# Fetching one of 112 gathered tiles row by row from the sync engine in a two-layer relational graph network

## The reference

```python
def rgcn_layer(x, src, dst, edge_type, w_rel, root, bias):     # N = 12500 nodes, E = 200000 edges, R = 10
    seg = dst * 10 + edge_type
    xs = x[src]                                                # one row of 128 floats for each edge
    sums = segment_sum(xs, seg, num_segments=N * 10)
    cnt = segment_sum(ones, seg, num_segments=N * 10)
    mean = (sums / maximum(cnt, 1.0)[:, None]).reshape(N, 10, 128)
    return einsum('nrd,rdo->no', mean, w_rel) + x @ root + bias

edge_type = argmax(edge_attr_42[:, 16:26], axis=1)
h = relu(rgcn_layer(x, src, dst, edge_type, w_rel1, root1, b1))
y = rgcn_layer(h, src, dst, edge_type, w_rel2, root2, b2)
out = layernorm(x + y)
```

## Time and profile before

| what | value |
|---|---|
| time, median of 3 runs | 3973.91 us (3973.23 to 3980.13) |
| the profiled execution's own time | 3973.67 us |
| its span, first to last instruction | 3972.0 us |
| busy share of the span: GpSimd, TensorE, VectorE, ScalarE | 75%, 67%, 47%, 9% |
| mean granted clock of TensorE | 0.819 of full speed |

### The profile page before, as it was taken

The page is one execution under the profiler, slowest core; times in us unless marked ns, Lnnn a source line. Parts: engine busy times, 40 slices in busy tenths (PEclk is TensorE's granted clock), DMA queues, the critical chain, the costliest instruction groups (busy, mean ns, idle before and its releaser), DMA issues.

```text
span 3972.0 us, 31733 instructions
## 1 busy us (share of the span) xinstructions
PE 2673.2 (67%) x10165; PEld 1797.6 (45%) x10166; DVE 1872.3 (47%) x2588; ACT 375.7 (9%) x399; POOL 2986.7 (75%) x3139
## 2 busy tenths in 40 slices
PE   4776777677677676777766666666666666666566
PEld 3444444444444444444454444444444444444444
DVE  6545545454554545555544343434434344443444
ACT  1010100101001010010100101010010100101010
POOL 7777777777777777777777777777777777777775
PEclk9787888878888888887888778788877878878788
DMA  4232232322323223232222222222222222222221
GB/s 132 75 88 84 78 94 78 90 79 78 94 78 94 74 78 94 78 88 67 80 67 61 66 62 63 62 65 62 63 63 65 63 62 62 65 62 63 64 64 52
DMA packets 151574, 293.69 MB, mean 74 GB/s; under 512 B 61619, under 2 KB 82503, under 8 KB 147958
## 3 DMA queue, kind: packets, MB, share of 16 engines
q0 software_dynamic: 100032, 205.07, 19.9%
q1 hardware_dynamic: 46630, 87.29, 6.7%
q10 hardware_dynamic: 4867, 0.79, 0.1%
HBM read 264.68 MB, written 28.25 MB: 74 GB/s over the span
## 4 chain that ended last, share of the span: by engine, by line
POOL 72%; issue 25%; PE 3%; POOLq 0%; DVE 0%; DMA 0%; ACT 0%; DVEq 0%
POOL rows L1400 71%; PE ps_agg L1820 1%; PE ps_agg L1817 1%; PE ps_out L1900 1%; PE ps_bc L1842 0%; DMA rows<-in_x_dram,idx_s 0%; POOLq L1436 0%; PE ps_agg L1900 0%; PE ps_out L1895 0%; DVE ring L2209 0%; DMA rows<-table,idx_s 0%; POOLq L1343 0%; POOLq L1430 0%; POOL mean L1396 0%; PE ps_out L1908 0%
## 5 line engine op out<-in xcount | busy, mean ns | idle before, releaser
L1400 POOL DMA_INDIRECT rows<-table,idx_s x1563 | 1481.7, 948 | 481.8 <-issue 481.8
L1400 POOL DMA_INDIRECT rows<-in_x_dram,idx_s x1507 | 1443.5, 958 | 459.3 <-issue 459.3
L1817 PE MATMUL ps_agg<-S_first,rows 128*128 128x390 f32 x1564 | 891.4, 660 | 1154.5 <-issue 727.9
L1820 PE MATMUL ps_agg<-S,rows 128*128 128x160 f32 (+2 forms) x4692 | 1241.1, 406 | 0.0
L2209 DVE TENSOR_TENSOR ring<-ps_agg,ring 128x429 f32 (+1 forms) x782 | 457.1, 585 | 1415.6 <-PE ps_agg L1820 696.7
L1820 PEld LDWEIGHTS ps_agg<-S,rows 128*128 128x128 f32 x4692 | 950.2, 242 | 347.7 <-issue 233.3
L1817 PEld LDWEIGHTS ps_agg<-S_first,rows 128*128 128x128 f32 x1564 | 336.5, 243 | 1397.2 <-issue 1022.8
L2195 DVE TENSOR_TENSOR S<-ps_iota,comb_b 128x1200 f32<-128x1200 f32 x392 | 547.5, 1397 | 0.0
L2253 DVE TENSOR_TENSOR mean<-ps_bc,ring 128x896 f32<-128x896 f32 (+2 forms) x284 | 300.7, 1060 | 490.8 <-PE ps_bc L1842 486.8
L1900 PE MATMUL ps_out<-mean,wall 128*128 128x448 f32 (+1 forms) x1120 | 507.9, 581 | 0.0
L1900 PEld LDWEIGHTS ps_out<-mean,wall 128*128 128x128 f32 x1120 | 228.9, 213 | 153.0 <-issue 143.9
(11 more groups left out here) (163 smaller groups left out, 814.6 us busy)
## 6 DMA issues: line engine op xcount, KB each, us to landing
attr<-in_edge_attr_dram SPq DMA_DIRECT2D x27, 1176.0 KB, 8.9
rows<-table,idx_s POOLq DMA_INDIRECT x1563, 2.5
rows<-in_x_dram,idx_s POOLq DMA_INDIRECT x1507, 2.5
x_in<-in_x_dram SPq DMA_DIRECT2D x54, 224.0 KB, 2.7
table<-h_s SPq DMA_DIRECT2D x54, 224.0 KB, 2.3
table<-outT SPq DMA_DIRECT2D x27, 224.0 KB, 3.7
xt_s<-table SPq DMA_DIRECT2D x27, 224.0 KB, 3.8
out_dram<-h_s SPq DMA_DIRECT2D x27, 224.0 KB
```

What stands on the lines that cost most here:

```text
L1400: pool.indirect_dma_start(out=rows[:, o, j, :], out_offset=None, in_=(x, table)[l][:, :], in_offset=bass.IndirectOffsetOnAxis(ap=at, axis= ...
L1817: ins = t_.matmul(sums, lhsT=rows[:, o, jj, :], rhs=S_first[:, PLACE[o], h, :, :], start=True, stop=False)
L1820: ins = t_.matmul(sums[:, :, lo:lo + w], lhsT=rows[:, o, jj, :], rhs=S[:, PLACE[o], h, j - 1, :].rearrange("p (r n) -> p r n", n=WN)[:, :, ...
```

## The change

For the first 13 laps of each layer the last tile of the lap, tile 7 of octet 6 in the odd half, is no longer gathered by GpSimd. The sync engine fetches it instead. A new function `fetch` runs four times in a lap, 32 rows each time, in a loop of four passes with eight rows a pass. A pass loads eight indices from `idx_sp` in SBUF into registers and issues eight DMAs. Each copies one row of 512 bytes from `x` or `htab` into `tile_d`, a scratch of 128 rows in DRAM. After the fourth part the sync engine waits until all 128 rows have landed, loads the whole scratch into `rows_sp` in SBUF, and loads the next lap's indices. TensorE takes this tile's weights from `rows_sp` and waits for `rows_sp_in` as well. The core of the diff:

```diff
+SP_OCT, SP_TILE, SP_LAPS, SP_UNIT, SP_PART = OCTS - 1, GT - 1, LAPS - 1, 8, 32
...
+        rows_sp = sb("rows_sp", [P, C])
+        idx_sp = sb("idx_sp", [1, P], I32)
...
+        tile_d = table2[60000:60000 + P, :]
...
+        def by_sync(b, par, o):
+            return par == 1 and o == SP_OCT and not is_(b, END)
...
-                            for j in range(GT - SHORT if is_(b, HALVES - 1) and o == OCTS - 1 else GT):
+                            for j in range(GT - SHORT if is_(b, HALVES - 1) and o == OCTS - 1 else
+                                           GT - 1 if by_sync(b, par, o) else GT):
...
+                def load_index(tile):
+                    sp.dma_start(idx_sp[0:1, :], src[bass.ds(tile * P, P)].rearrange("(a e) -> a e", a=1)
+                                 ).then_inc(idx_sp_in, 16)
+
+                def fetch(l, b, before, part):
+                    if isinstance(b, int) and b >= 2 * SP_LAPS:
+                        return
+                    if part == 0:
+                        landed = 8 * before + 16 * (1 - l)
+                        sp.wait_ge(idx_sp_in, landed if isinstance(b, int) else sp.snap(landed))
+                        if l or not is_(b, 0):
+                            sp.wait_ge(agg_ready[SP_OCT], before)
+                        if l and is_(b, 0):
+                            sp.wait_ge(rows_saved, 16 * PARTS)
+                        hold(b)
+                    with sp.Fori(part * SP_PART, (part + 1) * SP_PART - SP_UNIT + 1, SP_UNIT) as first:
+                        _, at = nc.values_load_multi_w_load_instructions(
+                            idx_sp[0:1, bass.ds(first, SP_UNIT)], engines=(SP_,), min_val=0, max_val=N - 1,
+                            skip_runtime_bounds_check_because=IN_ROWS)
+                        for e in range(SP_UNIT):
+                            sp.dma_start(tile_d[bass.ds(first + e, 1), :], (x, htab)[l][bass.ds(at[e], 1), :]
+                                         ).then_inc(row_copied[l], 16)
+                    if part == 3:
+                        copied = before * 1024 - l * (HALVES * 1024) + 1024
+                        sp.wait_ge(row_copied[l], copied if isinstance(b, int) else sp.snap(copied))
+                        hold(b)
+                        sp.dma_start(rows_sp[:, :], tile_d).then_inc(rows_sp_in, 16)
+                        if is_(b, 2 * SP_LAPS - 1):
+                            if l == 0:
+                                load_index(2 * HT - 1)
+                        else:
+                            load_index((b + 3) * HT - 1)
...
+                    fetch(0, b, before, 2 * par)
                     if not (isinstance(b, int) and b >= HALVES - 2):
                         sp.wait_ge(attr_used, with_it)
...
                         save_counts(b - 1, before)
+                    fetch(0, b, before, 2 * par + 1)
+                    if not is_(b, 0):
                         save_part(b - 1, 0, HN, before, h_s)
...
+                    fetch(1, b, before, 2 * par)
                     if not (isinstance(b, int) and b < 2):
                         save_out(b - 2, 0, HN, sp.snap(before - (HALVES + 1)) if not isinstance(b, int) else b - 1, o_s)
+                    fetch(1, b, before, 2 * par + 1)
                     sp.wait_ge(bc_ready[4], past)
...
+                            from_ = rows_sp[:, :] if by_sync(b, par, o) and jj == SP_TILE else rows[:, o, jj, :]
...
+                                    if par:
+                                        here = with_it * 8 - l * 16
+                                        pe.wait_ge(rows_sp_in, here if known else pe.snap(here))
```

More of the change, by code:

```diff
@@ L1117 @@
 DVE_ = mybir.EngineType.DVE
+IN_ROWS = "src names rows of x"
+SP_OCT, SP_TILE, SP_LAPS, SP_UNIT, SP_PART = OCTS - 1, GT - 1, LAPS - 1, 8, 32
+SP_ = mybir.EngineType.SP
 IN_RANGE = "the flag that chooses this path is computed from the same rows and bounds them"
@@ L1161, in gnn_kernel @@
         rows_in = [sem(f"rows_in{k}") for k in range(OCTS)]
+        row_copied = [sem(f"row_copied{l}") for l in range(2)]
+        rows_sp_in = sem("rows_sp_in")
+        idx_sp_in = sem("idx_sp_in")
         attr_max = sem("attr_max")
@@ L1567, in _ @@
                     load_late_src(o)
-                for b, before, with_it, par, past in halves(sp, 1, singly=1):
+                for b, before, with_it, par, past in halves(sp, 1, singly=2):
                     n = nodes_of(b)
+                    fetch(1, b, before, 2 * par)
                     if not (isinstance(b, int) and b < 2):
                         save_out(b - 2, 0, HN, sp.snap(before - (HALVES + 1)) if not isinstance(b, int) else b - 1, o_s)
+                    fetch(1, b, before, 2 * par + 1)
                     sp.wait_ge(bc_ready[4], past)
@@ L1819, in aggregate @@
                         else:
-                            ins = t_.matmul(sums[:, :, lo:lo + w], lhsT=rows[:, o, jj, :],
+                            from_ = rows_sp[:, :] if by_sync(b, par, o) and jj == SP_TILE else rows[:, o, jj, :]
+                            ins = t_.matmul(sums[:, :, lo:lo + w], lhsT=from_,
                                             rhs=S[:, PLACE[o], h, j - 1, :].rearrange("p (r n) -> p r n", n=WN)[:, :, 0:w],
@@ L1961, in _ @@
                             pe.wait_ge(S_ready[o], with_it)
-                            if o == OCTS - 1 and (l or last):
-                                gone = SHORT * 16 * (l + last)
-                                pe.wait_ge(rows_in[o], landed - gone if known else pe.snap(landed - gone))
+                            if o == OCTS - 1:
+                                if last:
+                                    gone = (l + 1) * (SHORT + SP_LAPS) * 16
+                                    pe.wait_ge(rows_in[o], landed - gone)
+                                else:
+                                    fixed = l * (SHORT + SP_LAPS) * 16 - l * HALVES * 8 - (1 - par) * 8
+                                    here = with_it * (P - 8) - fixed
+                                    pe.wait_ge(rows_in[o], here if known else pe.snap(here))
+                                    if par:
+                                        here = with_it * 8 - l * 16
+                                        pe.wait_ge(rows_sp_in, here if known else pe.snap(here))
                             elif l and is_(b, 0) and o < AHEAD:
```

## The result

The changed kernel takes 4039.62 us (median of 4 runs, 4038.61 to 4042.6) against 3976.26 for the kernel before in the same runs: 1.0162 times as long, 95% interval 1.0150 to 1.0174. It is 63 us slower; I had forecast it 33 faster, at 3941.

The account below looks back on a forecast made before the run. GpSimd, issuing gathers without pause, was taken to bound the kernel. Removing 13 gathers a layer saves 32.7 us from 3973.67, and the added work costs nothing: 3941 us predicted, own range 3937 to 3950, widened to 3936 to 3965.

Parts of the forecast that it names:

- The gathers do not get slower: Denies a rival: row copies beside GpSimd's gathers cost each 10 ns, 28 us of the gain, 3969 us; chance 0.05.
- Does it fit: Sync engine's work per lap against GpSimd's lap: 120 of 141.4 us in layer 0, 114 of 140.3 in layer 1.
- The row: One row copy on the sync engine: issue 0.475 plus 0.24 us for register instruction, moves and gaps, 0.71 in all.
- my limit of 31.7 for a part: Longest part of 32 rows that fits layer 0's lap: 31.7 us, a row of 0.88, an issue of 0.64.
- The old work: Sync engine's existing work in layer 0: 3.6 us for types and 2.1 for hidden rows each half, 11.4 a lap.
- 46 idle microseconds: TensorE idles about 46 us of each lap, so waiting 3.7 us for `rows_sp` once a lap was called free.
- the sum of 120: Sync engine in layer 0, per lap: four parts of 26.4 us plus 14.5 for old work, last landing and two issues.
- signs of being right: Gathers at 1.25 to 1.26 us, row issues 0.25 to 0.6, parts under 31, hidden-row stores slightly late, short `rows_sp` waits.
- the two of being wrong: GpSimd's sequencer waiting for TensorE in front of an octet; TensorE waiting tens of microseconds for `rows_sp`.
- the bounds: Limits for a row copy's issue on the sync engine: shortest plain issue 0.239 us, longest odd-shaped one 1.433.
- The sync engine becomes the bound: Rival: 128 row copies a lap decide from 0.88 us a row; 4441 us with an issue of 0.8; chance 0.14.
- TensorE's lateness comes back: Rival: TensorE over its 50 us makes GpSimd wait; 1.26 us a lap gives 3974, 2 gives 3993; chance 0.04.

Follow-up runs that it names:

- e9: The changed kernel with layer 0's attribute load issued behind the types' store and load back: 3943.31 us, ratio 0.9912 to the kernel before.
- e7: The changed kernel, but GpSimd gathers all 112 tiles, the sync engine's tile goes unused and part 0 waits for the scratch's readout: 3976.01 us, ratio 0.9998.
- e8: The changed kernel with the wait for octet 6 moved from part 0 to the load of `rows_sp`: 3983.78 us, ratio 1.0014 to the kernel before.
- e15: The changed kernel with each part's rows written out, only the source row from a register: 3936.67 us, ratio 0.9908 to the kernel before.
- e12: The changed kernel with rows copied straight into `rows_sp`, without scratch, on chips where the kernel before is slow: ratio 1.0459 to that kernel.
- e11: The changed kernel with rows written out into the scratch, on chips where the kernel before is slow: ratio 1.2092 to that kernel.
- e1: The changed kernel without row copies or scratch load, TensorE reading old rows, on slow chips: 4614 us against 4668 before, ratio 0.9881.

## Why the prediction was wrong

**What held.** GpSimd bounded the kernel, and the 26 gathers are worth what I said: 32.7 us forecast, 36.7 measured with direct copies (interval of the ratio 0.9893 to 0.9926, so 29 to 43). The DMA engines carry the packets without harm: queue q1 goes from 6.7 to 8.2% of their time, where I had 2% for the row copies. The gathers do not get slower, late types alone cost nothing, and in layer 1 the change does what was forecast.

**The step that failed is "Does it fit".** It added up the sync engine's work in layer 0 to 120 us a lap and held it against 141.4, the lap of 112 gathers, where the changed GpSimd has 111 and needs 140.1. The lap measured 147.9. Three terms make most of the difference, and the third is one of kind, not of size.

- The row. I took 0.71 us; it is 0.79 (issue 0.521 and not 0.475, register instruction 0.074 and not 0.06), and a part of 32 takes 29.4 and not 26.4: 12 us a lap. This alone stays under my limit of 31.7 for a part.
- The old work. I carried its 3.6 us for the types over unchanged, though its order had changed. The types' store now follows 32 row copies and the attributes at once, and the wait for it takes 5.0 instead of 1.3: 7.4 us a lap. e9 takes just this away.
- The closed circle. I let the tile be 3.7 us late and called it free, because TensorE has 46 idle microseconds and GpSimd gives it 50. I had part 0 wait "for the end of octet 6, about 1150", which is the old trace's 8 us of octet 6 behind 1142.3, although the line above it had the tile in SBUF only at 1146.0; and the sum of 120 has no term for this wait at all. But octet 6 itself waits for the tile that the parts bring. Once the tile is late, the wait is 5.4 us and moves along with the lateness, so it is a term of the sum, and the slack of TensorE does not pay for it. e7 and e8 take this one away.

With 120 + 12 + 7.4 + 5.4 the sum would have been 145, and about 3 us remain. Of the 147.9 four parts are 117.6, the waits for the types, the last row (13.2 / 11) and octet 6 are 10.0, 1.2 and 5.4, and 13.7 are left for the old issues with the holds and register instructions between them, for which my sum had about 10; for the last row's landing it had 2.3. The limit for a part was not 31.7 but about 27.5 (29.4 less a quarter of 7.8), between e15 with 25.1 and the change with 29.4.

So two of my signs of being right were seen in a kernel that is 63 us slower: issues of 0.521, within 0.25 to 0.6, and parts of 29.4, under 31. They rested on the same limit. The signs that told were the two of being wrong: GpSimd waiting for TensorE, and TensorE waiting 32.6 us a lap for `rows_sp`. A slip in the bounds changed nothing: the earlier trace rows has a plain issue of 1.751 us, longer than the 1.433 that I called the longest.

**Where the lost time shows.** A circle 7.8 us over GpSimd's lap makes TensorE later with each lap. GpSimd's lead of about 50 us hides the first laps; then it waits 7 to 10 us a lap, 83 in all, and at the end of the layer the rest of the lateness is paid once more, 20 us, at the restart. The prediction had no such term, and two of its sentences on what would be free ("out of 46 idle ones and 50 allowed") read a buffer as if it refilled.

**The rival that came.** "The sync engine becomes the bound" is what happened, by its mechanism in part: its place was right, its point of decision (a row of 0.88 us) and its price (4441) were not, since both rested on the same sum. "TensorE's lateness comes back" names the way in which the loss reached GpSimd, but it wanted parts of over 30 us, and its 1.26 to 2 us a lap in both layers were 6.4 in layer 0 (83.3 / 13) and none in layer 1.

A rule of the Trainium skill that I weighed there ("DMA: Bandwidth & Descriptors", Anatomy of one DMA: the fixed cost is mostly the wait for the write's receipt, in a fit that the page makes for DMAs of GpSimd) did not pace the copies: they start 0.79 us apart. It was near the truth in another place, the types' store to DRAM, whose landing stood inside the circle; that the attributes ahead of it set its length is what e9 shows.

## What to carry to other kernels

When an engine takes on work that another hands back to it (a buffer that is free only when the reader is done), add up the circle, landings and handoffs included, and hold it against the period; slack elsewhere hides lateness only once. Work that is moved in front of old work changes the landing times of the old work: put a store that is waited for ahead of the large load, not behind it. Wait for a handed-back buffer in front of the work that reads it, not in front of a whole group; here that is an advice from the trace and not from a run. And read the lateness at the end of a stage as well as inside it, since a buffer's lead is given back there.

## What the runs showed of the hardware that I had not expected

One row of 512 bytes takes 0.521 us to issue from DRAM to DRAM in 16 pieces, 0.513 with the target's place fixed, and 0.228 from DRAM into one partition of SBUF. So the shape of the copy sets the price, and the register hardly matters; whether it is the number of pieces or the kind of target was not separated.

On some chips the kernel before ran 17% slower, and in e12's trace there the sync engine's sequencer instructions stall for about 0.7 us. Programs with row copies lose more against the kernel before there: the looped ones 34 to 37%, the written out one 21% and the one with direct copies 4.6%, the last two 1% faster elsewhere. Their number of sync engine instructions alone does not say how much: e11 and e12 have nearly the same (11788 and 11718). e1, with hardly any (1201), has the "remote" waits of GpSimd all the same.
